# Draining the first layer's score strips earlier on VectorE, and two softmax steps on GpSimd instead of VectorE

## The reference, cut to what matters

```python
def _L0_attn_ref(x, Wq, bq, Wk, bk, Wv, bv, Wo, bo, slopes):
    ...
    scores = jnp.einsum('bhqd,bhkd->bhqk', q, k) / jnp.sqrt(jnp.float32(d))
    scores = scores + slopes[None, :, None, None] * dist[None, None]
    attn = jax.nn.softmax(scores, axis=-1)
    ctx = jnp.einsum('bhqk,bhkd->bhqd', attn, v)
    ...
x = x + _L0_xattn_ref(_layernorm(x), ctx_1024, ...)   # mean of the context, two products
x = x + _L0_attn_ref(_layernorm(x), ...)
x = x + _L0_ffn_ref(_layernorm(x), ...)               # shared SwiGLU and 8 routed experts
x = x + _L1_xattn_ref(_layernorm(x), ctx_1024, ...)   # 16 heads over 1601 keys: most of the work
x = x + _L1_attn_ref(_layernorm(x), ...)              # conv, gated scan, feed-forward
x = x + _L1_ffn_ref(_layernorm(x), ...)               # quantized MLP
```

## Time and profile before

| | us |
|---|---|
| median of 3 runs | 2205.45 (2204.77 to 2206.51) |
| profiled execution, its own time | 2202.09 |
| its span in the trace | 2200.3 |
| TensorE matmul busy | 1991.9 |
| VectorE busy | 1358.4 |
| ScalarE busy | 1051.9 |
| GpSimd busy | 558.7 |

### The profile page before, as it was taken

One profiled execution on the slowest core, in us unless ns is written; L12 is line 12 of the kernel. 1 busy time (PEld: TensorE's weight loads), 2 busy tenths in 40 slices (PEclk: granted clock), 3 DMA queues, 4 the chain that ended last, 5 costly groups with the idle time before them and its releaser, 6 DMA issues.

```text
span 2200.3 us, 72541 instructions
## 1 busy us (share of the span) xinstructions
PE 1991.9 (91%) x31814; PEld 1600.7 (73%) x31814; DVE 1358.4 (62%) x2525; ACT 1051.9 (48%) x1534; POOL 558.7 (25%) x966
## 2 busy tenths in 40 slices
PE   4788999999999999999999999999999988899977
PEld 3566777777878777777777777677787767777754
DVE  3456666756666667665656586575666676555533
ACT  2344445554455555445554544555554444444431
POOL 3222222322223132322223222232322222122101
PEclk9799999999999999999999999999999999999999
DMA  4443423343423343423233434143432320222121
GB/s 159 144 152 102 160 94 128 114 137 115 145 89 102 109 143 119 152 96 138 91 118 133 138 110 147 46 148 104 141 113 96 120 73 26 84 91 70 57 69 58
DMA packets 99256, 243.91 MB, mean 111 GB/s; under 512 B 13313, under 2 KB 19585, under 8 KB 98945
## 3 DMA queue, kind: packets, MB, share of 16 engines
q1 hardware_dynamic: 98944, 239.26, 32.0%
HBM read 235.94 MB, written 3.15 MB: 109 GB/s over the span
## 4 chain that ended last, share of the span: by engine, by line
PE 69%; DVE 16%; ACT 9%; issue 4%; SPq 1%; DMA 1%; POOL 0%; DVEq 0%; POOLq 0%; ACTq 0%
PE M L767 11%; PE SC L946 9%; PE M L774 9%; PE SC L969 7%; PE O L990 7%; ACT probT L1172 6%; DVE mx L1493 4%; PE X L796 4%; PE SC L962 3%; PE M L796 2%; PE X L1057 2%; PE M L837 2%; DVE oT L1505 1%; PE X L1028 1%; PE X L1045 1%
## 5 line engine op out<-in xcount | busy, mean ns | idle before, releaser
L1493 DVE TENSOR_REDUCE mx<-SC 128x4 f32<-128x1600 f32 (+1 forms) x256 | 466.5, 1822 | 137.2 <-PE SC L946 134.0
L1172 ACT ACTIVATE probT<-SC 128x2048 f32<-128x2048 f32 (+1 forms) x256 | 398.9, 1558 | 228.7 <-PE SC L969 227.7
L628 POOL TENSOR_TENSOR rowsT<-raw,rowsT 128x384 fp32r<-128x384 f32 (+1 forms) x256 | 281.6, 1121 | 485.7 <-ACT rowsT L1229 485.4
L774 PE MATMUL M<-wvs,rowsT 128*128 128x256 f32 x2496 | 360.2, 293 | 7.4 <-DVE SA L1337 5.8
L767 PE MATMUL M<-rowsT,wks 128*128 128x400 f32 (+1 forms) x1536 | 334.7, 362 | 20.7 <-DVE V L1313 14.7
L767 PEld LDWEIGHTS M<-rowsT,wks 128*128 128x128 f32 x1536 | 275.1, 192 | 96.8 <-issue 62.4
L774 PEld LDWEIGHTS M<-wvs,rowsT 128*128 128x128 f32 x2496 | 316.5, 193 | 27.1 <-DVE SA L1337 6.1
L1313 DVE TENSOR_TENSOR V<-M,bv 128x256 f32<-128x256 f32 (+1 forms) x448 | 159.9, 399 | 272.8 <-PE M L774 263.2
L1118 ACT ACTIVATE kT<-M,bk 128x400 f32<-128x400 f32 (+1 forms) x256 | 151.8, 595 | 365.7 <-PE M L767 365.1
L946 PE MATMUL SC<-kT,bdq 32*128 32x400 f32 (+1 forms) x2048 | 250.7, 557 | 49.5 <-ACT probT L1172 42.4
L990 PEld LDWEIGHTS O<-probT,V 128*17 128x17 f32 x13312 | 190.1, 98 | 70.8 <-issue 65.2
(11 more groups left out here) (253 smaller groups left out, 2443.5 us busy)
## 6 DMA issues: line engine op xcount, KB each, us to landing
ring<-in_ws_dram SPq DMA_DIRECT2D x428, 256.0 KB, 4.6
raw<-in_ctx_dram SPq DMA_DIRECT2D x32, 1601.0 KB, 8.1
summed<-in_ctx_dram SPq DMA_DIRECT2D x60, 800.5 KB, 4.5
ring<-rounded_scratch SPq DMA_DIRECT2D x64, 256.0 KB, 5.8
out_dram<-x SPq DMA_DIRECT2D x16, 128.0 KB, 2.8
kT<-in_ctx_dram SPq DMA_DIRECT2D x2, 800.5 KB, 8.6
x<-in_x_dram SPq DMA_DIRECT2D x11, 128.0 KB, 2.0
rounded_scratch<-wround SPq DMA_DIRECT2D x8, 128.0 KB, 2.2
```

The lines of the kernel that those rows point to most:

```text
L628: pool.tensor_tensor(rowsT[1][:, c, at], raw[:, c, at], rowsT[0][:, c, at], ALU.subtract).then_inc(low_ready, 1)
L774: mm = pe.matmul(bank[:, (t - 2 * a) * D:(t - 2 * a + 1) * D], rowsT[xp][:, cc, t * P:(t + 1) * P], wvs[wp][:, cc, :], start=(at == cc == ...
L1172: act.activation(probT[step % 3][0:w, :, 0:len(ts), :].rearrange("p j t q -> p j (t q)"), SC[0:w, :, 0:len(ts) * P], ACT.Exp)\
L1493: dve.tensor_reduce(mx[c][:, :, n], SC[:, :, 0:KCH[n][1]], AX.X, ALU.max).then_inc(max_used, 1)
```

## The change

VectorE drains the strips right behind the maxima of the slot, ahead of the copy of O and of the X drains of place C. The subtraction of the row maxima and the multiplication by the inverted sums leave VectorE. GpSimd does them, each at the very end of its slot (q = 6 and q = 7), behind two new semaphores. The shapes and the arithmetic are the same.

```diff
                     for t, q in second_layer(b, k):      # GpSimd, end of its slot
                         if q in (8, 9):
                             gates(t, q - 8)
+                    for i, q in first_layer(b, k):
+                        if q == 6:
+                            pool.wait_ge(rowmax_ready, i + 1)
+                            pool.tensor_tensor(SAs, SAs, rowmax[:, :].unsqueeze(2).to_broadcast([P, 16, S]), ALU.subtract).then_inc(shifted0, 1)
+                        if q == 7:
+                            pool.wait_ge(rowsum_ready, i + 1)
+                            pool.tensor_tensor(SAs, SAs, rowsum[:, :].unsqueeze(2).to_broadcast([P, 16, S]), ALU.mult).then_inc(p0_ready, 1)
...
                 def softmax_start(i):
                     wait_drained(dve, (i, "l0_s0", 0, 0))
                     wait_drained(dve, (i, "l0_s1", 0, 0))
-                    go(dve.tensor_reduce(rowmax[:, :], SAs, AX.X, ALU.max))
-                    dve.tensor_tensor(SAs, SAs, spread(rowmax[:, :], S), ALU.subtract).then_inc(shifted0, 1)
+                    dve.tensor_reduce(rowmax[:, :], SAs, AX.X, ALU.max).then_inc(rowmax_ready, 1)
 
                 def softmax_end(i):
                     dve.wait_ge(exp0, i + 1)
                     go(dve.tensor_reduce(rowsum[:, :], SAs, AX.X, ALU.add))
-                    go(dve.reciprocal(rowsum[:, :], rowsum[:, :]))
-                    dve.tensor_tensor(SAs, SAs, spread(rowsum[:, :], S), ALU.mult).then_inc(p0_ready, 1)
+                    dve.reciprocal(rowsum[:, :], rowsum[:, :]).then_inc(rowsum_ready, 1)
...
                     maxima(b, k)
+                    for what in pieces(b, k, "strips"):
+                        drain(what)
                     if k == 0 and 0 <= b - 1 < B:
                         dve.wait_ge(weighed, STEPS // 2 * b)
                         dve.tensor_copy(osb[:, :, :], Og).then_inc(o_used, 1)
                     for what in x_fills(b, k, "C"):
                         drain_x(what)
-                    for half in ("strips", "second"):
-                        for what in pieces(b, k, half):
-                            drain(what)
+                    for what in pieces(b, k, "second"):
+                        drain(what)
```

More of the change, by code:

```diff
@@ L465, in program @@
                                 "O0_ready", "th0_ready", "first_kept", "l0_done"))
+        rowmax_ready, rowsum_ready = sp.sem("rowmax_ready"), sp.sem("rowsum_ready")
         (score_shifted, score_exp, cnt_ready, onew_ready, tabs_ready, ex_tanh, hid_ready, experts_done) = (sp.sem(n) for n in (
```

## The result

The changed kernel takes 2185.22 us (median of 7 runs, 2180.33 to 2188.93) against 2204.77 us for the kernel before (7 runs, 2195.52 to 2206.52). The ratio is 0.9915 with an interval of [0.9897, 0.9934]: 18.7 us off, between 14.6 and 22.7. The forecast took 11.7 us off, and the range ended at 2187. So the sign was right, and the gain came out more than half again as large. Measured once more beside the last experiments, the changed kernel took 2187.71 us, ratio 0.9931 [0.9910, 0.9952]: 15.2 us off, between 10.6 and 19.8. That time is just inside the range, and that interval holds the 11.7. So the size of the miss is uncertain, and what decides where the prediction failed are the experiments on each part.

The account below looks back on a forecast made before the run. TensorE was taken as the bound, so only its waits count: 11.6 + 5.85 - 5.75 = 11.7 us off the profiled 2202.09 us gives 2190.4, or 2193.8 us for the median, range 2187 to 2204.

Parts of the forecast that it names:

- strips, 9 and 13: At softmax tiles 9 and 13 early strips end TensorE's stall before L774 and its low clock: 8.6 us off.
- strips, 5: At softmax tile 5 early strips end L767's 1.77 us stall and shorten the low clock: 1.7 us off.
- strips, 6, 10, 14: At these tiles strips no longer stand behind the copy of O, so small TensorE waits go: 1.3 us off.
- multiplication, 7, 11, 15: V drains behind the multiplication, for which L767 waits, come earlier: gains of 1.15, 1.35 and 1.15 us.
- multiplication, 5, 8, 9, 10, 12: Behind the multiplication: 0 on balance at 8, 0.25 us given back at 12, no gain named at 5, 9 and 10.
- subtraction, 2, 3, 8, 10, 12: Held VectorE operations or later exp at these tiles: losses of 1.0, 1.0, 0, 1.0 and 0.75 us.
- tile 0: The subtraction stands behind four L628, and the first transpose L851 already waits for the multiplication: 1.5 us lost.
- tile 13: L1552, a two-input VectorE operation, is held and TensorE waits for the maxima behind it: 0.5 us lost.
- Part 1: VectorE drains the strips right behind the maxima, which adds no work: 11.6 us off in all.
- the first rival: The clock falls at tiles 9 and 13 all the same: gain 4.6 us instead of 8.6, 2197.8 us; chance 0.10.
- Part 2: Subtraction and multiplication go to GpSimd at 2.35 us each: 5.85 us gained, 5.75 us lost.
- The slower rival by the port: New GpSimd instructions hold two-input VectorE operations, each passing 1.1 us to TensorE: up to 2222 us; chance 0.09.

Follow-up runs that it names:

- strips at 9 and 13: Kernel before with strips drained right behind the maxima at tiles 9 and 13 only, softmax steps on VectorE: 2194.87 us, ratio 0.9976 to the kernel before.
- strips alone: Kernel before with strips drained right behind the maxima at all tiles, subtraction and multiplication on VectorE: 2193.55 us, ratio 0.9958 to the kernel before.
- strips with subtraction: Kernel before with early strips and only the subtraction on GpSimd, multiplication on VectorE: 2194.92 us, ratio 0.9968 to the kernel before.
- multiplication alone: Kernel before with only the multiplication on GpSimd, strips drained late: 2192.04 us, ratio 0.9953 to the kernel before.
- changed kernel again: The changed kernel without edit, measured a second time: 2187.71 us, ratio 0.9931 to the kernel before.
- strips with multiplication: Kernel before with early strips and only the multiplication on GpSimd, subtraction on VectorE: 2177.94 us, ratio 0.9891; once more on another chip 2182.02 us, 0.9909.
- four pairs: Four comparisons of kernels that differ only by the subtraction on GpSimd: it costs 5.3, 4.8, 2.2 and 6.2 us by the ratios.
- Halves: The changed kernel with the subtraction and the multiplication each as two GpSimd instructions of 512 columns: 2182.18 us, ratio 0.9912 to the kernel before.

## Why the prediction was right about one part and wrong about the other

The steps of the pipeline, from the traces, beside the terms of the sum (us off; a minus is a loss; places where the clock fell in one of the two traces are left out):

| place | forecast | measured | trace |
|---|---|---|---|
| strips, 9 and 13 | 8.6 | 8.6 | strips at 9 and 13 |
| strips, 5 | 1.7 | 2.0 | strips alone (5.93) less strips at 9 and 13 (3.89) |
| strips, 6, 10, 14 | 1.3 | 2.3 | strips alone; at 14 strips with subtraction |
| multiplication, 7, 11, 15 | 3.65 | 3.6 | multiplication alone |
| multiplication, 6 and 14 | 1.9 | 1.3 | multiplication alone |
| multiplication, 4 | 0.3 | 1.05 | multiplication alone |
| multiplication, 5, 8, 9, 10, 12 | inside losses, or 0 | 2.8 | multiplication alone |
| subtraction, 2, 3, 8, 10, 12 | -3.75, the multiplication's share in it | -1.9 | changed kernel again less strips with multiplication |
| tile 0 | -1.5 | -0.75 here, 0 to -1.1 elsewhere | wait of L859 for the multiplication |
| tile 13 | -0.5 | 0 | no wait of TensorE behind L1305 |

**Part 1** held by its own steps. L774 waits for no strips at 9 and 13, rb is the next to be late (1.65 us, where I had 1.2), and the clock came back. The trace of the kernel before, and the two others in which the strips are drained late, show the clock at 0.50 at both places, six times in six. In the eleven traces with early strips it is so twice in twenty-two. So the first rival, that the clock falls all the same, is out as a rule. One of the two is tile 13 in the first trace of the changed kernel, behind the longest of the gaps named above (1.33 us); its value products took 2.80 us there. The other is tile 9 in strips with the multiplication, behind the 1.65 us for rb. Gaps of up to 1.06 us at 13, and the same wait for rb at 9, stand in other traces without a fall, so what sets it off is open. The gap also moves the step at 13, which is 3.54 us with a gap of 1.06 and 4.46 with 0.15: its size here, 3.83, is that of one execution. Tile 5 came out right by luck: the 10.2 us of low clock in the earlier trace rows belong to that one execution. No other trace has more than 3.4 us there. The two in the table have none, differ at tile 5 by the early strips, and lie 2.0 us apart there, near the stall of 1.77.

**Part 2** is the step that failed: gains of 5.85 us against losses of 5.75 ("Together 5.75"), so nothing on balance. The losses were too large and the gains too small: the multiplication alone took 10.3 us off, and the subtraction cost 4.6 us in the mean of four pairs. Three things in it were wrong.

1. The duration. An estimate that carried the slope of 256 and 512 columns on to 1024 gave 2.35 us; the trace shows 1.90. L628 was not a good measure: for 512 columns the new operation takes 1.04 us beside its 1.30. The two differ in the output type (L628 writes fp32r) and in the second input (a broadcast in the new one), and no run sets these apart. At tile 3, where I had a loss of 1.0, exp waits 4.27 us in the changed kernel, less than the 4.37 of the earlier trace rows, and the place loses nothing:

```profile
325.56 1.06 ACT L1276 ACTIVATE SA<-SA 128x1024 f32<-128x1024 f32 x1 [4.27 <-POOL SA L755]
```

2. The hold. That it exists and lasts for the whole instruction was right. What it costs was wrong, because I charged the hold and didn't credit VectorE with the 1.24 us of the subtraction that it no longer does just before. At tile 12 L1440 takes 1.62 us instead of 0.17, and 1.45 - 1.24 is 0.2 us: L970's wait for the maxima is 1.61 us against 1.43 in the earlier trace rows. At 8 it is 0.2 too, and at 2 the first of the two holds costs 2.27 - 0.75 - 1.24 = 0.3, the trace says 0.30. At 13 L1305 takes 2.00 instead of 0.40 and nobody waits. Only tiles 2 and 10 pay more, 0.9 and 0.7 in all. Tile 12 in the changed kernel:

```profile
1301.43 1.90 POOL L755 TENSOR_TENSOR SA<-SA,rowmax 128x1024 f32<-128x1024 f32 x1 [10.37 <-DVE rowmax L1380]
...
1301.73 1.62 DVE L1440 TENSOR_TENSOR cnt<-cnt,cntg 128x8 f32<-128x8 f32 x1
...
1307.06 0.25 PE L970 MATMUL SC<-mT,sel 32*65 32x128 bf16 x4 [1.61 <-DVE mx L1499]
```

3. The gains behind the multiplication. I looked at the wait right behind it and took 1.15 where TensorE waited. I missed that GpSimd's own low part moves behind the multiplication and stops holding VectorE: I had named that at tile 11, and saw it nowhere else; at 8 it takes 1.12 us off the routing's operation, and TensorE's wait of 1.25 us for V is gone. At 4, 5, 10 and 12 the drains and the maxima behind the multiplication simply come forward, where I had a loss, a third of this, or nothing. The six tiles that I had counted sum to 5.9, as forecast (5.85), by errors that cancel; the missed ones are 2.8.

With the measured steps the sum is 12.9 + 8.75 - 1.9 - 0.75 = 19.0 us, beside 18.7 and, the second time, 15.2 measured. The agreement with the first is closer than the parts are, and in part luck: by the times part 1 is 9.2 us (up to 12.5) where its steps say 12.9, and the subtraction costs 4.6 where its steps say 1.9.

The slower rival by the port is refuted. Section 4.1 of the GPSIMD Engine Reference in the Trainium skill, which sends elementwise work to VectorE, doesn't hold for the multiplication: moving it to the slower engine (1.90 us instead of 1.25) took 10.3 us off. For the subtraction the rule holds, 4.6 us lost. What separates them, as far as the rows show, is who waits. In the kernel before, the first transpose started 1.27 us or more after the multiplication at fourteen of sixteen tiles; exp started within 0.04 us of the subtraction's end at four (3, 8, 10 and 12), and at others the routing and the rounding stand on VectorE beside it. Halves speak for the held operations rather than for the late exp: with them exp gets its scores 0.17 us later still, and the time falls by 4.0 us. But halves changed both steps, so that is argued and not shown for the subtraction alone. The Trainium skill (SBUF — State Buffer, "Who interferes with whom") calls the shared port pair an exclusive lock. The traces agree: the end of the held operation moved by 0.86 us when the GpSimd instruction became 0.86 us shorter. It also says that a `tensor_scalar` can contend and that a `tensor_reduce` never does on this chip. Both are seen: L1305, a TENSOR_SCALAR with one SBUF tensor as input, went from 0.40 to 2.00 us, and the reductions of 1024 columns took 1.19 to 1.22 us in both kernels.

**What stays open.** The subtraction's steps sum to 1.9 us, its time to 4.6. Low clock is a candidate for the rest: between 330 and 2060 us the six kernels with the subtraction on GpSimd at fifteen or sixteen tiles have the clock at 0.50 for 4.3 times 3.4 us on average, the seven others with a part of the change 2.7. (Each group holds one kernel with late strips, with three such stretches at 9 and 13.) At 1.6 us each the difference is 2.6 us. But one trace of each kernel is little. Many stretches come back at a few places, near the strips of tile 5 in seven of the fourteen traces and near 1340 us behind the wait for rb in six, but at none of them in every trace. The clearest is tile 7, where the changed kernel loses 1.6 us in its second trace without any wait ahead of it that the other kernel lacks; strips with subtraction loses the same there, and none of the other twelve traces does. TensorE's products there, in the changed kernel and in the one without the subtraction:

```profile
728.44 0.95 PE L954 MATMUL SC<-kT,bdq 32*128 32x400 f32 x8 [0.25 <-ACT probT L1180]
729.19 2.22 PE L845 MATMUL M<-PT 32*128 32x64 f32 x32
731.34 3.54 PE L998 MATMUL O<-probT,V 128*17 128x64 f32 x128
```

```profile
730.42 0.95 PE L956 MATMUL SC<-kT,bdq 32*128 32x400 f32 x8 [0.25 <-ACT probT L1182]
731.16 2.20 PE L847 MATMUL M<-PT 32*128 32x64 f32 x32
733.30 1.98 PE L1000 MATMUL O<-probT,V 128*17 128x64 f32 x128
```

The same 128 products take 3.54 us and 1.98, and the window of the first shows why, the granted clock of 0.51:

```profile
731.20:734.60 3.40, 3.40 (x128) 3.31 (x130) 1.37 (x3) 0.00 (x0) 0.99 (x1) 0.51 0.03 7
```

Whether the subtraction causes such stretches, or these six traces only had more of them, is not shown.

## What to carry to other kernels

Price a move between engines on both queues. The operations that follow the moved one on its new engine move too, and if they hold up operations of the old engine, as the low part did here, their place may be worth more than the work that left. Before moving elementwise work to GpSimd, look at what waits for the result: the multiplication, with 1.27 us or more before its transposes at nearly all tiles, gained; the subtraction, with exp right behind it at some, lost. And where a long GpSimd instruction must run beside VectorE operations with their inputs in SBUF, try to split it: here two halves cost 0.17 us more and released VectorE 0.86 us sooner.

## What the runs showed of the hardware

- GpSimd's elementwise operation on 128x1024 fp32 with a broadcast second input took 1.90 us in the median of the 32 instructions (2.08 at most, beside the rounding on VectorE), on 128x512 1.04 us. The difference is 1.68 ns per column, with 0.18 us left over: an estimate from two sizes.
- VectorE is held even for a tiny operation: 8 columns took 1.63 us instead of 0.17, and one input in SBUF is enough (L1305, 0.40 to 2.00 us). A small operation ends within 0.05 us of the GpSimd instruction that was running, the rounding 0.54 us after it, and in the halves a held operation ends behind the first of the two without waiting for the second.
- TensorE's clock stood at 0.50 for 3.4 us at places that differ from one execution to the next, in three cases with no wait of 0.3 us or more in the 9 us ahead of them, 1.6 us each. A step of this size in one trace is no finding before a second trace shows it.
- A gap of TensorE before L998 at tile 13 that the profile puts down to no releaser was 0.15 to 1.33 us long in the fourteen traces, 0.79 and 1.33 in two executions of one kernel.
